# Gated products of a feed-forward on GpSimd in place of VectorE, with a copy by ScalarE

## Chip, cores and metric

One core of one Trainium2 chip. The metric is the device time of one execution in microseconds. The core has five queues that matter here: TensorE (PE in the profile; PEld are its weight loads), VectorE (DVE), ScalarE (ACT), GpSimd (POOL) and SyncE (SP), which issues the DMAs. Each runs its instructions strictly in order and waits for the others on semaphores.

## What is computed

`x` is 8 sequences of 512 tokens of width 128, float32. First comes a recurrent layer (`h = tanh(h A' + x B')`, output `h C'`, with layer norms and a residual), 512 steps one after the other. Then six layers, each of a local attention and a gated feed-forward:

```python
for i in range(DEPTH):                                   # DEPTH = 6
    x = attn_layer(shift_tokens(x), Wqkv[i], q_scale[i], k_scale[i], Wo[i]) + x
    x = ffn_layer(shift_tokens(x), ln_g[i], ln_b[i], W1[i], b1[i], W2[i], b2[i]) + x

def attn_layer(x, Wqkv, qs, ksc, Wo):                    # 16 heads of 64, windows of 32 tokens
    q, k, v = split(x @ Wqkv)
    q, k = rotate(l2norm(q) * qs), rotate(l2norm(k) * ksc)
    return local_attention(q, k, v) @ Wo                 # softmax over this window and the one before

def ffn_layer(x, g, bln, W1, b1, W2, b2):                # inner width 341
    xn = layernorm(x) * g + bln
    a, gate = jnp.split(xn @ W1 + b1, 2, -1)
    return a * jax.nn.gelu(gate, approximate=False) @ W2 + b2
```

## The kernel before

The order of the work is written out by hand for each engine; there is no planner. After the recurrence (about the first 400 us of the span) all six layers run as one software pipeline over 192 attention tiles (`NT`): 6 layers x 8 chunks of 64 tokens x 4 tiles; a tile is 4 sequences x 32 tokens = 128 rows. On each engine `step(s)` does one stage each of up to four tiles: A = s (projection of q and k, rotation, squares), B = s - 1 (normalised q and k transposed, scores, maximum), C = s - 2 (exponential, sum, weighting, product with the inputs), E = s - 3 (the output projection L597 and its addition to the residual). Four tiles are a turn T: 512 columns (8 sequences x 64 tokens, `CH`) that then go through the feed-forward. `turn_of(s, lag)` gives the turn whose feed-forward stage with that lag falls in step s:

- s mod 4 = 3, lag 7 and 11: rows transposed (L522), statistics on VectorE (`statistics`, L877, L881), small sums on GpSimd (L433, L435), and of the turn before, value product 0 (L544, then `glu`, L869).
- s mod 4 = 0, lag 8 and 12: GpSimd's shift (L408), ScalarE's normalised rows (L724); of the turn before, value products 1 and 2 (L544, `glu`).
- s mod 4 = 1, lag 9 and 13: transposed back and scaled (L529, L730); of the turn before, the output product (L551) and VectorE's update of the residual (`update`, L887).
- s mod 4 = 2, lag 6 and 10: the feed-forward's input is copied (L698); the gates (L537) and their Gelu on ScalarE (`gelu`, L741).

The inner width of 341 is held in three pieces of 128, 128 and 85 partitions (`FT`), so each turn has three gates `ge`, three values and three products `hh`, each 512 columns wide. Values come from TensorE in PSUM: `VALUES = ((11, 0, 2), (12, 1, 1), (12, 2, 2))` gives lag, piece and bank. PSUM has eight banks. Banks 4 to 7, named G(0) to G(3), are shared in each step by the transposed q and k (L509), the feed-forward's products, and the product with the inputs (L657). So L657 of tile C must wait until each bank has been read by its feed-forward user (`ffn_left`, called ahead of the first matmul into each bank, in the order 3, 0, 1, 2). `glu` on VectorE reads the value from PSUM, adds the bias, multiplies by the gate and writes `hh`; it counts `glu_done`, for which TensorE waits in `ffn_left` and ahead of L551.

VectorE's order in a step: rotation of q (L845, L848), sum of the exponentials (L906) and its reciprocal (L909), square sum of q (L854), residual (L914), rotation of k (L845, L848), transpose of the weights (L921), statistics, `glu` 0 or `glu` 1, `update`, square sum of k (L854), maximum of the scores (L938), `glu` 2, subtraction of the maximum (L944), inverse roots (L859 and L55 to L65, eleven small instructions one behind the other). ScalarE's: L749 (empties what L657 wrote), inputs L698, exponential L755, square of q (L709), L760, transposed q and k out of PSUM (L770, L775), `gelu` 0, square of k (L709), `ffn`. GpSimd's: shift L408, q and k times inverse roots (L414), weights (L419), q and k rotations added (L424), tables (L397), small sums (L433, L435). The inverse roots wait for L433 where there are statistics in the step (`variance_done`).

Of the kernel before, what the change touches and what calls it, by code (L numbers as in the profile page):

```python
# [104 lines left out]
def build(nc, a):  # L105
    with ExitStack() as ctx:
        def sb(name, shape, dt=F32):
            return ctx.enter_context(nc.sbuf_tensor(name, shape, dt))

        def sem(name):  # L110
            return ctx.enter_context(nc.semaphore(name))
# [45 lines left out]
        nmean = sb("nmean", [P, TB])  # L157
        ge = sb("ge", [P, 3, CH])
        hh = sb("hh", [P, 3, CH])

        mask_f = ex
        flat = cosp.rearrange("p a c n -> p (a c n)")
# [88 lines left out]
        gate_done = sem("gate_done")  # L251
        gelu_done = sem("gelu_done")
        a_done = sem("a_done")
        glu_done = sem("glu_done")
        fy_done = sem("fy_done")
        x_updated = sem("x_updated")
# [6 lines left out]
        def tile(n):  # L263
            return 0 <= n < NT

        def turn_of(s, lag):
            T = (s - lag) // ROUND
            return T if (s - lag) % ROUND == 0 and 0 <= T < TURNS else None

# [112 lines left out]
        @block.gpsimd  # L382
        def _(eng):
            eng.memset(xa[:, :, 0:1], 0.0).then_inc(zeroed, 1)
            eng.memset(xb[:, :, 0:1], 0.0).then_inc(zeroed, 1)
            eng.memset(hb[:, 1, FW - 1, :], 0.0).then_inc(zeroed, 1)
            eng.memset(kT[:, :, :, :, :], 0.0).then_inc(zeroed, 1)
            eng.memset(xtm[:, :, :, :], 0.0).then_inc(zeroed, 1)

            for c in range(NC):  # L390
                eng.wait_ge(h_done, FW * c + FW)
                after(eng, hs_turned, c)
                eng.tensor_copy(hs.rearrange("p (b t) -> p b t", b=BATCH), hb[:, c % 2, :, :].rearrange("p t b -> p b t")).then_inc(hs_done, 1)

            def scale_table(w, T):
                eng.wait_ge(tab_in[w], 32 * (T + 1))
                eng.tensor_tensor(tab[:, w, :, :], tab[:, w, :, :], qks[:, w, :, :], ALU.mult).then_inc(tab_ready[w], 1)  # L397

            scale_table(0, 0)

            def step(s):
                A, B, C = s, s - 1, s - 2
                T = turn_of(s, 8)
                if T is not None:
                    eng.wait_ge(norm_step, normed(s) if s <= NT else normed(s) + NSTEPS + 1)
                    after(eng, xn_ready, TB * T)
                    eng.wait_ge(variance_done, 2 * T + 2)
                    eng.tensor_tensor(shift[:, :], nmean[:, :], rr[:, 1, 2 * HEADS:], ALU.mult).then_inc(shift_done, 1)  # L408
                if tile(B):
                    eng.wait_ge(norm_step, normed(B + 1))  # L410
                    for i in range(2):
                        eng.wait_ge(rot_added, 2 * B + i + 1)
                        v = cosp[:, B % 2, i, :].rearrange("p (h d) -> p h d", d=DH)
                        eng.tensor_tensor(v, v, rr[:, B % 2, HEADS * i:HEADS * i + HEADS].unsqueeze(2).to_broadcast([P, HEADS, DH]),  # L414
                                          ALU.mult).then_inc(rot_ready, 1)
                if tile(C):
                    eng.wait_ge(recip_done, C + 1)
                    after(eng, p_turned, C)
                    eng.tensor_tensor(pn[:, :].rearrange("p (h k) -> p h k", k=DH), ex[:, :].rearrange("p (h k) -> p h k", k=DH),  # L419
                                      rsum[:, :].unsqueeze(2).to_broadcast([P, HEADS, DH]), ALU.mult).then_inc(weighed, 1)  # L420
                if tile(A):
                    for i, roped in enumerate((q_roped, k_roped)):
                        eng.wait_ge(roped, 2 * A + 2)
                        eng.tensor_tensor(cosp[:, A % 2, i, :], cosp[:, A % 2, i, :], sinp[:, i, :], ALU.add).then_inc(rot_added, 1)  # L424
                    if A % ROUND == 1:
                        scale_table(1, A // ROUND)
                    if A % ROUND == 3 and A + 1 < NT:
                        scale_table(0, A // ROUND + 1)
                T = turn_of(s, 7)
                if T is not None:  # L430
                    eng.wait_ge(stat_step, 2 * TB * T + 2 * TB)
                    after(eng, norm_step, normed(s))
                    eng.tensor_scalar(ss[:, 2 * HEADS:], aggr[:, :, 1], EPS, None, ALU.add).then_inc(variance_done, 1)  # L433
                    after(eng, shift_done, T)
                    eng.tensor_scalar(nmean[:, :], aggr[:, :, 0], -1.0, None, ALU.mult).then_inc(variance_done, 1)  # L435

            for s in range(LAST):
                step(s)

        @block.tensor  # L440
        def _(eng):
# [112 lines left out]
            def ffn_left(s, k):  # L554
# [9 lines left out]
                for lag, m, bank in VALUES:  # L564
                    T = turn_of(s, lag)
                    if T is not None and k == bank:
                        eng.wait_ge(glu_done, 3 * T + m + 1)
                T = turn_of(s, 13)
                if T is not None and k == 2:
                    eng.wait_ge(x_updated, NC + T + 1)  # L570
# [99 lines left out]
        def _(eng):  # L670
# [65 lines left out]
            def gelu(T, m):  # L736
# [3 lines left out]
                eng.wait_ge(gate_done, 3 * T + m + 1)  # L740
                eng.activation(ge[0:fn, m, :], G(GATE_BANKS[m])[0:fn], ACT.Gelu, bias=vec[0:fn, 6 + m:7 + m]).then_inc(gelu_done, 1)  # L741

            def step(s):
                A, B, C, E = s, s - 1, s - 2, s - 3
                if tile(E):
# [30 lines left out]
                T = turn_of(s, 10)  # L776
                if T is not None:
                    gelu(T, 0)
                if tile(A):
                    square(A, 1)  # L780
                ffn(s)
# [19 lines left out]
        def _(eng):  # L801
# [58 lines left out]
                eng.wait_ge(norm_step, base + 1)  # L860
                rsqrt(eng, ss[:, lo:hi], rbits[:, lo:hi], rhalf[:, lo:hi], rr[:, s % 2, lo:hi], norm_step, base + 1)

            def glu(T, m, k):
                fn = FT[m][1]
                eng.wait_ge(w1_in, 16 * DMA_W1 * (T // NC + 1))
                eng.wait_ge(a_done, 3 * T + m + 1)
                eng.wait_ge(gelu_done, 3 * T + m + 1)
                after(eng, fy_done, T)
                eng.scalar_tensor_tensor(out=hh[0:fn, m, :], in0=G(k)[0:fn], scalar=vec[0:fn, 3 + m:4 + m], in1=ge[0:fn, m, :],  # L869
                                         op0=ALU.add, op1=ALU.mult).then_inc(glu_done, 1)  # L870

            def statistics(T):
                base = 2 * TB * T
                eng.wait_ge(rows_done, T + 1)
# [22 lines left out]
            def step(s):  # L897
# [20 lines left out]
                if tile(C):  # L918
                    eng.wait_ge(weighed, C + 1)
                    after(eng, px_done, 4 * C)  # L920
                    eng.transpose(pT[:, :], pn[:, :]).then_inc(p_turned, 1)  # L921
                T7, T11, T12, T13 = turn_of(s, 7), turn_of(s, 11), turn_of(s, 12), turn_of(s, 13)
                if T7 is not None:
                    statistics(T7)
                if T11 is not None:
                    glu(T11, 0, 2)
                if T12 is not None:
                    glu(T12, 1, 1)
                if T13 is not None:
                    update(T13)  # L930
                c = leaving(s)
# [4 lines left out]
                if tile(B):  # L936
                    eng.wait_ge(sims_done, B + 1)
                    eng.tensor_reduce(mx[:, :], S, AX_X, ALU.max).then_inc(max_done, 1)  # L938
                if T12 is not None:
                    glu(T12, 2, 2)  # L940
                if tile(B):
                    eng.wait_ge(max_done, B + 1)
                    after(eng, exp_done, B)
# [76 lines left out]
```

## Time and profile before

| | us |
|---|---|
| timed runs, median of 3 (lowest, highest) | 3785.27 (3783.42, 3791.43) |
| the profiled execution | 3787.83 |
| its span, first to last instruction | 3786.0 |
| TensorE busy | 3558.4 |
| VectorE busy | 3058.2 |
| GpSimd busy | 2086.7 |
| ScalarE busy | 2037.8 |
| mean granted clock of TensorE | 0.969 of full speed |

Busy time is the sum of an engine's instructions; matmuls are pipelined, so a busy TensorE may still be a slow one. The profile puts an engine's idle time down to what released it: the instruction of another engine whose semaphore came last, or "issue" where nothing of the kind is seen. The timeline gives start and duration of merged instructions, the granted clock is a mean over the stretch asked for, 1.00 being full speed.

### The profile page before, as it was taken

Reading aid. Unit: us, or ns where it says so; the run is one execution under the profiler, and the core shown is the slowest. Engines: PE = TensorE matmul, PEld = TensorE weight load, DVE = VectorE, ACT = ScalarE, POOL = GpSimd, SP = SyncE. Lnnn points to the kernel's source line nnn. Section 1 sums busy time; section 2 is a strip of 40 time slices with the busy share of each in tenths; the row PEclk is TensorE's granted clock in tenths of the full one; section 3 lists DMA queues with packets and bytes.
Section 4 is the critical chain, followed back from the end, with each engine's and each line's share of the span. In section 5 each row is a group of like instructions: output and inputs, shape, how many; then the busy total and the mean of one; then the engine's idle time right before and its main releaser. Section 6 shows DMA issues by size and latency. Waiting matters only on the chain.

```text
span 3786.0 us, 101581 instructions
## 1 busy us (share of the span) xinstructions
PE 3558.4 (94%) x42643; PEld 2250.6 (59%) x42643; DVE 3058.2 (81%) x5670; ACT 2037.8 (54%) x3871; POOL 2086.7 (55%) x1217
## 2 busy tenths in 40 slices
PE   8999699999999999999999999999999999999997
PEld 4555366666665666666665666666656666566664
DVE  3443698888898888888888898888888888888884
ACT  2222356565565565565655655656556556556553
POOL 0000376666566666666665666666666666666662
PEclk9999899999999999999999999999999999999998
DMA  2000000000001000001000001000001000000000
GB/s 66 1 1 1 7 10 12 28 10 10 9 14 32 10 10 7 10 16 29 10 10 10 7 16 32 10 7 10 10 15 31 10 10 7 14 12 16 10 10 12
DMA packets 62283, 52.55 MB, mean 14 GB/s; under 512 B 11526, under 2 KB 59396, under 8 KB 61828
## 3 DMA queue, kind: packets, MB, share of 16 engines
q1 hardware_dynamic: 61828, 46.05, 4.6%
q8 instruction: 338, 5.54, 0.6%
q14 instruction: 117, 0.96, 0.1%
HBM read 43.93 MB, written 2.10 MB: 12 GB/s over the span
## 4 chain that ended last, share of the span: by engine, by line
PE 62%; DVE 19%; issue 11%; POOL 5%; ACT 2%; DVEq 0%; DMA 0%; SPq 0%; POOLq 0%; ACTq 0%
PE ps L502 16%; PE ps L597 12%; PE ps L657 7%; PE ps L469 6%; PE ps L509 6%; DVE sinp L848 4%; DVE mx L938 3%; PE ps L643 3%; PE ps L551 3%; DVE pT L921 3%; PE ps L485 3%; PE ps L537 3%; POOL cosp L424 2%; POOL cosp L414 2%; DVE ss L854 2%
## 5 line engine op out<-in xcount | busy, mean ns | idle before, releaser
L414 POOL TENSOR_TENSOR cosp<-cosp,rr 128x1024 f32<-128x1024 f32 x384 | 722.5, 1902 | 823.1 <-DVE rr L65 823.0
L424 POOL TENSOR_TENSOR cosp<-cosp,sinp 128x1024 f32<-128x1024 f32 x384 | 904.7, 2368 | 96.1 <-DVE sinp L848 95.5
L502 PE MATMUL ps<-w_qk,xs 128*128 128x512 f32 x1536 | 814.9, 656 | 19.8 <-ACT sq L709 14.2
L597 PEld LDWEIGHTS ps<-px,w_vo 128*128 128x128 f32 x6144 | 729.5, 197 | 155.2 <-issue 118.7
L597 PE MATMUL ps<-px,w_vo 128*128 128x128 f32 x6144 | 739.6, 280 | 22.9 <-issue 18.4
L709 ACT ACTIVATE sq<-ps 128x1024 f32<-128x1024 f32 x384 | 393.1, 1024 | 571.3 <-DVE sinp L848 571.3
L845 DVE TENSOR_TENSOR cosp<-ps,tab 128x1024 f32<-128x1024 f32 x384 | 469.6, 1223 | 267.6 <-PE ps L502 267.4
L749 ACT COPY px<-ps 128x512 f32<-128x512 f32 x768 | 398.8, 598 | 431.0 <-PE ps L657 428.2
L657 PE MATMUL ps<-pT,xtm 32*128 32x512 f32 x3072 | 539.6, 629 | 88.3 <-DVE hh L869 74.7
L502 PEld LDWEIGHTS ps<-w_qk,xs 128*128 128x128 f32 x1536 | 279.9, 203 | 403.5 <-issue 401.8
L854 DVE TENSOR_REDUCE ss<-sq 128x16 f32<-128x1024 f32 x384 | 455.6, 1187 | 60.9 <-ACT sq L709 60.5
L848 DVE TENSOR_TENSOR sinp<-ps,tab 128x1024 f32<-128x1024 f32 x384 | 466.3, 1214 | 0.0
L509 PEld LDWEIGHTS ps<-ident,cosp 128*128 128x128 f32 x3072 | 352.2, 142 | 159.4 <-issue 101.0
L509 PE MATMUL ps<-ident,cosp 128*128 128x128 f32 x3072 | 403.4, 275 | 43.5 <-POOL cosp L414 31.1
L419 POOL TENSOR_TENSOR pn<-ex,rsum 128x1024 f32<-128x1024 f32 x192 | 365.1, 1902 | 98.1 <-DVE rsum L909 98.1
L657 PEld LDWEIGHTS ps<-pT,xtm 32*128 32x128 f32 x3072 | 202.1, 184 | 274.4 <-DVE hh L869 113.2
L775 ACT COPY kT<-ps 128x512 f32<-128x512 f32 x384 | 206.1, 589 | 279.4 <-PE ps L509 279.4
L643 PEld LDWEIGHTS ps<-kT,qT 64*32 64x32 f32 x24576 | 254.6, 105 | 84.5 <-issue 78.0
L469 PE MATMUL ps<-ident_bf 128*128 128x512 bf16 x1024 | 303.8, 377 | 0.0
L643 PE MATMUL ps<-kT,qT 64*32 64x64 f32 x24576 | 286.0, 226 | 2.2 <-ACT kT L775 2.1
L485 PEld LDWEIGHTS ps<-cosp,qT 128*128 128x128 f32 x1024 | 154.0, 189 | 166.4 <-ACT cosp L688 156.1
L921 DVE STREAM_TRANSPOSE pT<-pn 128x1024 f32<-128x1024 f32 x192 | 237.0, 1234 | 3.5 <-POOL pn L419 3.5
(101 smaller groups left out, 4094.2 us busy)
## 6 DMA issues: line engine op xcount, KB each, us to landing
tab<-in_tab SPq DMA_DIRECT2D x96, 128.0 KB, 2.0
qks<-in_scales SPq DMA_DIRECT2D x96, 128.0 KB, 3.2
w_qk<-in_L_ffn_Wqkv SPq DMA_DIRECT2D x12, 512.0 KB, 6.9
w_v<-in_wv_t SPq DMA_DIRECT2D x6, 512.0 KB, 8.7
w_o<-in_L_ffn_Wo SPq DMA_DIRECT2D x6, 512.0 KB, 9.1
x<-in_L_attn_x SPq DMA_DIRECT2D x16, 128.0 KB, 3.4
out<-w_v SPq DMA_DIRECT2D x16, 128.0 KB, 2.4
w<-in_L_ffn_W SPq DMA_DIRECT2D x6, 341.0 KB
```

What stands on the lines that cost most here:

```text
L414: eng.tensor_tensor(v, v, rr[:, B % 2, HEADS * i:HEADS * i + HEADS].unsqueeze(2).to_broadcast([P, HEADS, DH]), ALU.mult).then_inc(rot_read ...
L424: eng.tensor_tensor(cosp[:, A % 2, i, :], cosp[:, A % 2, i, :], sinp[:, i, :], ALU.add).then_inc(rot_added, 1)
L469: eng.matmul(ps[:, 7, 0:KEEP].rearrange("p (a n) -> p a n", n=P), ident_bf[:, :], ident_bf[:, :].unsqueeze(1).to_broadcast([P, KEEP // P, ...
L502: t = eng.matmul(ps[:, u, :], xs[:, n % ROUND, :], w_qk[:, n // TILES % 2, i, 512 * u:512 * u + 512], start=True, stop=True)
L509: t = eng.transpose(G(k)[:, 128 * m:128 * m + 128], cosp[:, n % 2, i, at:at + 128], ident[:, :])
L597: t = eng.matmul(S0, w_vo[:, i // HP, i % HP, :], px[:, i, :], start=i == 0, stop=i == HEADS - 1)
L643: t = eng.matmul(ps[32 * b:32 * b + 32, 2 + h2, DH * hp:DH * hp + DH], qT[rows, hp, 32 * b:32 * b + 32], kT[rows, B % NG, hp, b, :], start ...
L657: t = eng.matmul(G(b), xtm[rows, C % NG, k, :], pT[rows, :].rearrange("p (h k q) -> p h k q", k=2, q=WIN)[:, :, k, :], start=k == 0, stop= ...
L749: eng.copy(px[:, :, 32 * b:32 * b + 32], G(b).rearrange("p (h q) -> p h q", q=WIN)).then_inc(px_evac, 1)
L845: eng.tensor_tensor(cosp[:, n % 2, i, :].rearrange("p (h d) -> p h d", d=DH), src, cos, ALU.mult).then_inc(roped, 1)
L848: eng.tensor_tensor(sinp[:, i, :].rearrange("p (h u f) -> p h u f", u=2, f=32), swapped, sin, ALU.mult).then_inc(roped, 1)
L854: eng.tensor_reduce(ss[:, HEADS * i:HEADS * i + HEADS], sq[:, i, :].rearrange("p (h d) -> p h d", d=DH), AX_X, ALU.add).then_inc(ssq_done, 1)
```

## The change

The buffer `aa` is added in SBUF. ScalarE copies each value with its bias from PSUM into `aa` (`value`, an Identity activation), behind its copies of q and k and ahead of the square of k, and counts `a_out`. GpSimd multiplies `aa` by the gate `ge` into `hh`, behind its additions for q and k and its table product, and counts `glu_done`. `glu` leaves VectorE. TensorE's `ffn_left` waits for `a_out` in place of `glu_done`; its wait ahead of L551 stays on `glu_done`. No DMA is added or moved; the load of W1 still waits for `glu_done`.

```diff
--- before.py
+++ after.py
@@ -157,6 +157,7 @@
         nmean = sb("nmean", [P, TB])
         ge = sb("ge", [P, 3, CH])
         hh = sb("hh", [P, 3, CH])
+        aa = sb("aa", [P, 3, CH])
 
         mask_f = ex
         flat = cosp.rearrange("p a c n -> p (a c n)")
@@ -251,6 +252,7 @@
         gate_done = sem("gate_done")
         gelu_done = sem("gelu_done")
         a_done = sem("a_done")
+        a_out = sem("a_out")
         glu_done = sem("glu_done")
         fy_done = sem("fy_done")
         x_updated = sem("x_updated")
@@ -426,6 +428,14 @@
                         scale_table(1, A // ROUND)
                     if A % ROUND == 3 and A + 1 < NT:
                         scale_table(0, A // ROUND + 1)
+                for lag, m, k in VALUES:
+                    T = turn_of(s, lag)
+                    if T is not None:
+                        fn = FT[m][1]
+                        eng.wait_ge(a_out, 3 * T + m + 1)
+                        eng.wait_ge(gelu_done, 3 * T + m + 1)
+                        after(eng, fy_done, T)
+                        eng.tensor_tensor(hh[0:fn, m, :], aa[0:fn, m, :], ge[0:fn, m, :], ALU.mult).then_inc(glu_done, 1)
                 T = turn_of(s, 7)
                 if T is not None:
                     eng.wait_ge(stat_step, 2 * TB * T + 2 * TB)
@@ -564,7 +574,7 @@
                 for lag, m, bank in VALUES:
                     T = turn_of(s, lag)
                     if T is not None and k == bank:
-                        eng.wait_ge(glu_done, 3 * T + m + 1)
+                        eng.wait_ge(a_out, 3 * T + m + 1)
                 T = turn_of(s, 13)
                 if T is not None and k == 2:
                     eng.wait_ge(x_updated, NC + T + 1)
@@ -740,6 +750,13 @@
                 eng.wait_ge(gate_done, 3 * T + m + 1)
                 eng.activation(ge[0:fn, m, :], G(GATE_BANKS[m])[0:fn], ACT.Gelu, bias=vec[0:fn, 6 + m:7 + m]).then_inc(gelu_done, 1)
 
+            def value(T, m, k):
+                f0, fn = FT[m]
+                eng.wait_ge(w1_in, 16 * DMA_W1 * (T // NC + 1))
+                eng.wait_ge(a_done, 3 * T + m + 1)
+                after(eng, glu_done, 3 * T)
+                eng.activation(aa[0:fn, m, :], G(k)[0:fn], ACT.Identity, bias=vec[0:fn, 3 + m:4 + m]).then_inc(a_out, 1)
+
             def step(s):
                 A, B, C, E = s, s - 1, s - 2, s - 3
                 if tile(E):
@@ -776,6 +793,10 @@
                 T = turn_of(s, 10)
                 if T is not None:
                     gelu(T, 0)
+                for lag, m, k in VALUES:
+                    T = turn_of(s, lag)
+                    if T is not None:
+                        value(T, m, k)
                 if tile(A):
                     square(A, 1)
                 ffn(s)
@@ -859,15 +880,6 @@
                 eng.tensor_scalar(ss[:, lo:hi], ss[:, lo:hi], 1e-24, None, ALU.max).then_inc(norm_step, 1)
                 eng.wait_ge(norm_step, base + 1)
                 rsqrt(eng, ss[:, lo:hi], rbits[:, lo:hi], rhalf[:, lo:hi], rr[:, s % 2, lo:hi], norm_step, base + 1)
-
-            def glu(T, m, k):
-                fn = FT[m][1]
-                eng.wait_ge(w1_in, 16 * DMA_W1 * (T // NC + 1))
-                eng.wait_ge(a_done, 3 * T + m + 1)
-                eng.wait_ge(gelu_done, 3 * T + m + 1)
-                after(eng, fy_done, T)
-                eng.scalar_tensor_tensor(out=hh[0:fn, m, :], in0=G(k)[0:fn], scalar=vec[0:fn, 3 + m:4 + m], in1=ge[0:fn, m, :],
-                                         op0=ALU.add, op1=ALU.mult).then_inc(glu_done, 1)
 
             def statistics(T):
                 base = 2 * TB * T
@@ -919,13 +931,9 @@
                     eng.wait_ge(weighed, C + 1)
                     after(eng, px_done, 4 * C)
                     eng.transpose(pT[:, :], pn[:, :]).then_inc(p_turned, 1)
-                T7, T11, T12, T13 = turn_of(s, 7), turn_of(s, 11), turn_of(s, 12), turn_of(s, 13)
+                T7, T13 = turn_of(s, 7), turn_of(s, 13)
                 if T7 is not None:
                     statistics(T7)
-                if T11 is not None:
-                    glu(T11, 0, 2)
-                if T12 is not None:
-                    glu(T12, 1, 1)
                 if T13 is not None:
                     update(T13)
                 c = leaving(s)
@@ -936,8 +944,6 @@
                 if tile(B):
                     eng.wait_ge(sims_done, B + 1)
                     eng.tensor_reduce(mx[:, :], S, AX_X, ALU.max).then_inc(max_done, 1)
-                if T12 is not None:
-                    glu(T12, 2, 2)
                 if tile(B):
                     eng.wait_ge(max_done, B + 1)
                     after(eng, exp_done, B)
```

## Rows read from the trace of the kernel before

**Rows 1.** The page, part 1: busy time, share of the span and instructions of each engine.

```profile
PE 3558.4 (94%) x42643; PEld 2250.6 (59%) x42643; DVE 3058.2 (81%) x5670; ACT 2037.8 (54%) x3871; POOL 2086.7 (55%) x1217
```

**Rows 2.** Timeline (start us, us, engine line op out<-in xcount), the output update, three successive turns.

```profile
2149.95 0.75 DVE L887 SCALAR_TENSOR_TENSOR xa<-ps,vec,xb 128x512 f32<-128x512 f32 x1 [0.46 <-PE ps L551]
...
2216.85 0.75 DVE L887 SCALAR_TENSOR_TENSOR xa<-ps,vec,xb 128x512 f32<-128x512 f32 x1 [0.47 <-PE ps L551]
...
2287.08 0.75 DVE L887 SCALAR_TENSOR_TENSOR xa<-ps,vec,xb 128x512 f32<-128x512 f32 x1 [0.46 <-PE ps L551]
...
2355.67 0.75 DVE L887 SCALAR_TENSOR_TENSOR xa<-ps,vec,xb 128x512 f32<-128x512 f32 x1 [0.46 <-PE ps L551]
```

**Rows 3.** Timeline of TensorE: an update step's L657, then a value step; [idle before <-releaser].

```profile
2009.41 2.00 PE L657 MATMUL ps<-pT,xtm 32*128 32x512 f32 x16
...
2054.00 1.88 PE L544 MATMUL ps<-xf,w 128*128 128x512 f32 x4
...
2057.65 1.13 PE L657 MATMUL ps<-pT,xtm 32*128 32x512 f32 x6
...
2060.43 2.27 PE L657 MATMUL ps<-pT,xtm 32*128 32x512 f32 x10 [1.64 <-DVE hh L869]
...
2062.63 3.35 PE L502 MATMUL ps<-w_qk,xs 128*128 128x512 f32 x4
```

**Rows 4.** Waits: who waited for whom, us in total, times, longest us.

```profile
PE ps L657 <- DVE hh L869: 74.7, 46, 1.6
```

**Rows 5.** Windows: start:end, length, busy time of each engine, granted clock (PEclk), DMA share, GB/s.

```profile
2062.60:2066.00 3.40, 3.40 (x7) 1.58 (x7) 1.26 (x7) 2.63 (x6) 1.85 (x1) 0.59 0.03 5
```

**Rows 6.** Timeline of ScalarE, VectorE and GpSimd, a statistics step.

```profile
2038.93 1.02 ACT L709 ACTIVATE sq<-ps 128x1024 f32<-128x1024 f32 x1 [0.88 <-DVE sinp L848]
...
2041.05 0.75 DVE L869 SCALAR_TENSOR_TENSOR hh<-ps,vec,ge 128x512 f32<-128x512 f32 x1
...
2041.71 1.21 DVE L854 TENSOR_REDUCE ss<-sq 128x16 f32<-128x1024 f32 x1
...
2042.20 0.23 POOL L433 TENSOR_SCALAR ss<-aggr 128x4 f32<-128x4 f32 x1
```

**Rows 7.** Timeline of VectorE, the value step that follows.

```profile
2056.76 0.71 DVE L869 SCALAR_TENSOR_TENSOR hh<-ps,vec,ge 128x512 f32<-128x512 f32 x1
...
2057.39 1.21 DVE L854 TENSOR_REDUCE ss<-sq 128x16 f32<-128x1024 f32 x1
...
2059.64 0.74 DVE L869 SCALAR_TENSOR_TENSOR hh<-ps,vec,ge 85x512 f32<-85x512 f32 x1
...
2060.30 1.21 DVE L944 TENSOR_TENSOR sh<-ps,mx 128x1024 f32<-128x1024 f32 x1
```

**Rows 8.** Groups by line: xcount | busy us, mean ns | idle before us <-releasers.

```profile
L424 POOL TENSOR_TENSOR cosp<-cosp,sinp 128x1024 f32<-128x1024 f32 x384 | 904.7, 2368 | 96.1 <-DVE sinp L848 95.5
...
L741 ACT ACTIVATE ge<-ps,vec 128x512 f32<-128x512 f32 x144 | 93.1, 687 | 1.6 <-PE ps L537 1.0
...
L397 POOL TENSOR_TENSOR tab<-tab,qks 128x256 f32<-128x256 f32 x96 | 70.0, 729 | 0.0
...
L730 ACT ACTIVATE xf<-ps,vec 128x512 f32<-128x512 f32 x48 | 37.1, 772 | 1.7 <-PE ps L529 1.7
```

**Rows 9.** Timeline of ScalarE and GpSimd, the same value step.

```profile
2053.73 4.70 POOL L424 TENSOR_TENSOR cosp<-cosp,sinp 128x1024 f32<-128x1024 f32 x2
...
2055.72 1.02 ACT L709 ACTIVATE sq<-ps 128x1024 f32<-128x1024 f32 x1 [0.88 <-DVE sinp L848]
...
2064.14 3.76 POOL L414 TENSOR_TENSOR cosp<-cosp,rr 128x1024 f32<-128x1024 f32 x2 [5.72 <-DVE rr L65]
```

**Rows 10.** Timeline of VectorE, L845 in a value step at full clock.

```profile
2195.57 1.22 DVE L845 TENSOR_TENSOR cosp<-ps,tab 128x1024 f32<-128x1024 f32 x1 [0.52 <-PE ps L502]
...
2206.61 1.23 DVE L845 TENSOR_TENSOR cosp<-ps,tab 128x1024 f32<-128x1024 f32 x1 [0.31 <-PE ps L502]
...
2212.88 1.23 DVE L845 TENSOR_TENSOR cosp<-ps,tab 128x1024 f32<-128x1024 f32 x1 [1.23 <-PE ps L502]
```

## Prediction, written before the changed kernel was run

> **What bounds the kernel now.** I read the page first, then the groups by line, then the waits, then the instructions in order of time for one turn, and last the granted clock of short stretches. On the page [rows 1] TensorE is busy for 94% of the span; but a busy TensorE is not one at full speed, and the same row has VectorE at 81%. So I looked at whole turns (four steps of the pipeline, one feed-forward turn in them). The output update at L887 runs once a turn, and its starts [rows 2] give the length of three successive turns: 2216.85 - 2149.95 = 66.90 us, then 70.23, then 68.59. Leaving aside turns that load a new layer and the last ones, whose steps also turn results out, all come in these three lengths: one fixed schedule with something of 0, about 1.67 or about 3.32 us on top.
>
> I name the steps by the feed-forward work in them: gate step (L537, L741), statistics step (L877, value product 0), value step (value products 1 and 2), update step (L551, L887). The extra time is all in the value step. There TensorE's last product of attention, L657, is cut in two [rows 3]: six matmuls start at 2057.65, ten at 2060.43, after 1.64 us of idling "<-DVE hh L869". In the waits this pair is 74.7 us in 46 waits [rows 4]: it happens in every turn. What comes behind it differs: in that turn the next projection L502 takes 3.35 us, and the stretch 2062.6 to 2066 has a granted clock of 0.59 of full speed [rows 3, 5], that is a mixture of the 2.4 GHz level and the 1.2 GHz level. The engine had been idle for 1.64 us just before the fall. So the feed-forward products on VectorE cost twice: TensorE waits for them, and in most turns it then runs slow for some us, in which VectorE waits for TensorE.
>
> **What the change removes from the statistics step.** The one L869 there starts at 2041.05 and the next square sum L854 at 2041.71 [rows 6]: 0.66 us of VectorE's queue. From there to the next step VectorE doesn't idle, so all of it should come off the step if nothing else becomes late. ScalarE gets the value copy in front of the square of k. That square runs from 2038.93 to 2039.95 [rows 6]; behind a copy of 0.7 us it ends near 2040.6, and L854 can start at 2041.05 at the earliest, so nearly 0.5 us remain. 45 such steps: 45 x 0.66 = 29.7 us.
>
> **What it removes from the value step.** Here VectorE has two L869: 2056.76 to 2057.39 = 0.63, and 2059.64 to 2060.30 = 0.66 us of its queue [rows 7]. The second stands behind the maximum in VectorE's queue, and TensorE's L657 needs bank 2 empty: that is the stall. After the change L657 waits for ScalarE's copy. TensorE's four L544 matmuls for both values run from 2054.00 to 2055.88 [rows 3]; the first copy can start near 2055.0, the second near 2056.0. A copy is an ACTIVATE with a bias from PSUM: L741 with a Gelu takes 687 ns, L730 with bias and scale 772 [rows 8]. I take 0.69 and keep 0.77 as the long end; the second, ending near 2056.7, is done 0.95 us before L657 starts at 2057.65. So L657 runs in one piece, 2.00 us as in the update step [rows 3], and there is no stall.
>
> The price is that the square of k, which starts at 2055.72 and takes 1.02 us [rows 9], now starts behind both copies, near 2056.65, and ends near 2057.7. VectorE's L854 needs it. It started at 2057.39; without the first product it would be ready at 2056.76, but now waits until 2057.7, that is 0.31 us later than today. The second product's 0.66 us then come off: 0.35 us earlier at L944, of which I keep 0.3, since the maximum is then read by the very next instruction. So of 1.29 us taken from VectorE in this step only 0.3 are won there, and 0.94 turn into a wait for ScalarE. (With a copy of 0.77 us the win is 0.2; if the copies delay nothing, 1.29.)
>
> Now the TensorE side, first in a turn at full clock. From L845 for k at 2195.57 to the same in the next step at 2212.88 are 17.31 us [rows 10]. In it VectorE waits for TensorE 0.31 us at 2206.61 and 1.23 at 2212.88, where 0.52 is the ordinary wait at this place (the first of these rows); both waits come from the late L657. Without the stall 17.31 - 0.31 - (1.23 - 0.52) = 16.29, less 0.3 = 15.99 us. So 1.32 us a turn, 45 turns: 59.4 us. Next limits: after L657, ScalarE's normalising activations L724 end about 1 us later than now (the copies before them), and L749, which empties what L657 writes, can begin when L657 ends; by my estimate TensorE is then ready for the next step about 0.5 us before VectorE needs it. Little, but enough.
>
> Then the clock. I counted the value steps by length, from L845 to L845: of 45, 10 have 17.3 us, 19 have 19.0 and 16 have 20.6 (the differences are those of the turns in rows 2). If the clock doesn't fall any more, 19 x 1.67 + 16 x 3.32 = 84.8 us are won. TensorE's other, shorter waits are there now in the turns that keep their clock as well, so I expect no fall from them.
>
> **What it adds to GpSimd.** Three tensor-tensor products of 512 columns a turn. L424 (both inputs full tensors, 1024 columns) takes 2368 ns, L397 (256 columns) 729 [rows 8]. A line through both is 0.18 us + 2.13 ns a column, 1.27 us for 512; half of L424 is 1.18, twice L397 1.46, the two ends. They stand behind both L424. In the value step these end at 2053.73 + 4.70 = 2058.43, the two products at 2061.0; the next need of GpSimd is L414 at 2064.14, 0.35 earlier after the change [rows 9]. Nearly 3 us are to spare. In the statistics step the product stands behind L424 and L397 and ahead of L433, whose result VectorE's inverse root waits for: L433 started at 2042.20 [rows 6] and starts near 2043.5 now. VectorE needs it after L854, L938 and L944; in the value step these take 2060.30 - 2057.39 - 0.66 = 2.25 us up to L944 and 1.21 for that one [rows 7], so near 2041.05 + 3.46 = 2044.5. Some 0.8 us are to spare when L433 itself is added. The products' reader, L551, comes a step later. I cost all three at nothing. The cover in the statistics step is the thinner one: a product of over 2.1 us would show there.
>
> The Trainium skill ("SBUF — State Buffer", "Who interferes with whom") speaks against moving work there: a VectorE instruction with two SBUF inputs and a GpSimd instruction that reads SBUF exclude one another for the whole instruction. No row of before has the two at once. In VectorE's order only the small instructions of the inverse roots (L61 to L65) have two such inputs, and they start 0.8 us after the products' end. By the rule nothing changes unless the products are later than worked out; that is the second rival.
>
> **Ends of the run.** In the last two turns nothing hides the products: copy and product in a row (0.69 + 1.27) for 0.73, the second product behind the first. I add 2.5 us.
>
> **Sum.** 29.7 + 59.4 + 84.8 - 2.5 = 171.4 us. The profiled execution took 3787.83 us around a span of 3786.0; the three timed runs have a median of 3785.27, 2.6 us lower; I take the sum off the median: 3785.3 - 171.4 = 3614 us, 4.5% faster.
>
> **Rivals.** (1) The clock still falls, though the stall is gone. For it: the stall alone doesn't decide it, since 10 of the 45 value steps have the same stall and keep the clock. Against: all slow L502 that I found stand behind the cut L657. Of the 84.8 us some 0.5 us a fall are then hidden by the slack found above, 35 x 0.5 = 17; so 68 us are not won: 3682 us. Chance 0.14.
> (2) GpSimd's products fall on VectorE's inverse roots, or the two hold each other up, up to one product a turn: 48 x 1.27 = 61 us less won, 3675 us. For it: GpSimd's queue is in order and a product could start late. Against: the margins of 0.8 us. Chance 0.06.
> (3) Slower than before: GpSimd becomes the bound. A product of X us delays the statistics step by X - 2.1 and the value step, with two, by 2X - 5.4. The gain of 171.4 / 48 = 3.6 us a turn is used up at 3X - 7.5 = 3.6, X = 3.7 us; at X = 4 the kernel takes 48 x 0.9 = 43 us more, 3828. Against it stand L424 and L397: X is three times what they give. Chance 0.03.
> (4) The change doesn't do what it says: L657 goes on waiting at the same place, for ScalarE's copies, since they are later than I make them by more than 2.5 us, and the time stays within 0.2%. For it nothing but the longer queue of ScalarE, which is 54% busy [rows 1]. Chance 0.02.
>
> **How the numbers follow.** The forecast holds with 0.75. Its own spread: copies at 0.77 us cost 5 us, the square not being late would win 45 x 1.0 = 45, but needs TensorE to be early as well (at most the 0.5 us, 22 us): 3592 to 3625. The range reaches to both middling rivals: 3592 to 3690. Differences under 0.2% (about 8 us) can't be told from none. Faster 0.95, same 0.02, slower 0.03.
>
> **What would show it.** L657 in one piece of 16 matmuls in the value step, and no wait of it for VectorE; granted clock near 1.00 through the value step; L869 gone from VectorE, a new wait of L854 for the square of nearly 1 us once a turn; GpSimd products near 1.27 us with no wait of L414 or of the inverse roots behind them; turns of one length near 66.9 - 1.3 - 0.66 = 64.9 us. It would be wrong if slow projections remained, if L657 waited for a copy, or if the inverse roots waited for L433.

## The result

The changed kernel takes 3610.27 us (median of 4 runs, 3609.73 to 3610.63) against 3785.3 before: a ratio of 0.9535, 95% interval 0.9518 to 0.9551. The forecast was 3614 us. Span 3608.3 us, mean granted clock 0.992 in place of 0.969. The page, part 1 (busy us, share, instructions), against rows 1 of before:

```profile
PE 3439.6 (95%) x42643; PEld 2181.2 (60%) x42643; DVE 2965.6 (82%) x5526; ACT 2116.0 (59%) x4015; POOL 2260.2 (63%) x1361
```

VectorE lost 93 us of work, ScalarE and GpSimd got 78 and 174. TensorE's busy time fell by 119 us though it does the same 42643 matmuls; by lines, L657 went from 539.6 to 459.0 us and the projection from 814.9 to 761.1. Only a part of that is the clock: in `e4_filled` below, at full clock but with L657 still waiting, the two have 515.0 and 757.8 us. The rest of L657's fall is that its matmuls no longer wait in between. The output update L887 is now L899; three of its starts (start us, us), answering to rows 2:

```profile
1862.18 0.75 DVE L899 SCALAR_TENSOR_TENSOR xa<-ps,vec,xb 128x512 f32<-128x512 f32 x1 [0.46 <-PE ps L561]
...
1926.95 0.75 DVE L899 SCALAR_TENSOR_TENSOR xa<-ps,vec,xb 128x512 f32<-128x512 f32 x1 [0.46 <-PE ps L561]
...
1991.68 0.75 DVE L899 SCALAR_TENSOR_TENSOR xa<-ps,vec,xb 128x512 f32<-128x512 f32 x1 [0.46 <-PE ps L561]
```

64.77 and 64.73 us: the turns have one length now (those that load a new layer and the last ones apart), where before they had 66.9, 68.6 or 70.2. From the first update to the 45th the run of before took 3045.8 us, this one 2870.3: 175.5 us for 44 turns, 3.99 a turn.

A value step of the changed kernel, from its timeline (start us, us, engine, line), answering to rows 3, 7 and 9. L554 are the value matmuls, L758 the copies, L438 the products, L719 the square, L875 the square sum, L667 what was L657, L512 the projection, L880 the first instruction of the inverse roots, L866 the next rotation:

```profile
1972.48 1.88 PE L554 MATMUL ps<-xf,w 128*128 128x512 f32 x4
...
1973.60 0.69 ACT L758 ACTIVATE aa<-ps,vec 128x512 f32<-128x512 f32 x1 [0.27 <-issue]
...
1974.45 0.68 ACT L758 ACTIVATE aa<-ps,vec 85x512 f32<-85x512 f32 x1 [0.17 <-PE ps L554]
...
1975.04 1.01 ACT L719 ACTIVATE sq<-ps 128x1024 f32<-128x1024 f32 x1
...
1976.08 1.22 DVE L875 TENSOR_REDUCE ss<-sq 128x16 f32<-128x1024 f32 x1 [0.76 <-ACT sq L719]
...
1976.14 2.00 PE L667 MATMUL ps<-pT,xtm 32*128 32x512 f32 x16
...
1976.85 2.51 POOL L438 TENSOR_TENSOR hh<-aa,ge 128x512 f32<-128x512 f32 x2
...
1978.07 1.98 PE L512 MATMUL ps<-w_qk,xs 128*128 128x512 f32 x4
...
1978.47 1.22 DVE L950 TENSOR_TENSOR sh<-ps,mx 128x1024 f32<-128x1024 f32 x1
...
1979.61 0.17 DVE L880 TENSOR_SCALAR ss<-ss 128x32 f32<-128x32 f32 x1
...
1982.16 1.22 DVE L866 TENSOR_TENSOR cosp<-ps,tab 128x1024 f32<-128x1024 f32 x1
```

The reader is to see three things. L667 runs in one piece of 16 matmuls and the projection behind it takes 1.98 us, not 3.35: no stall, full clock. L875 has a new wait of 0.76 us for the square that now stands behind the copies. And GpSimd's two products end at 1979.36, only 0.25 us before VectorE's L880 starts. The statistics step, answering to rows 6:

```profile
1957.96 0.69 ACT L758 ACTIVATE aa<-ps,vec 128x512 f32<-128x512 f32 x1 [0.71 <-issue]
...
1960.22 1.18 DVE L875 TENSOR_REDUCE ss<-sq 128x16 f32<-128x1024 f32 x1
1961.33 1.21 DVE L946 TENSOR_REDUCE mx<-ps 128x16 f32<-128x1024 f32 x1
...
1961.28 1.27 POOL L438 TENSOR_TENSOR hh<-aa,ge 128x512 f32<-128x512 f32 x1
...
1962.63 0.23 POOL L443 TENSOR_SCALAR ss<-aggr 128x4 f32<-128x4 f32 x1
...
1963.71 0.17 DVE L880 TENSOR_SCALAR ss<-ss 128x36 f32<-128x36 f32 x1
```

L875 follows the statistics without a wait, and L443 ends 0.85 us before L880 needs it. The granted clock over 1000 us in the middle (the column behind POOL's) is full:

```profile
1500.00:2500.00 1000.00, 976.27 (x12978) 630.22 (x12977) 897.79 (x1616) 642.62 (x1114) 723.59 (x436) 1.00 0.06 15
```

### The profile page after: what moved, and what is told of

It reads as the page before. It is cut to its first block and busy times, and to the rows that moved or that the text cites. A ratio compares the mean times of both kernels' runs of the same rounds, so it can differ in the third digit from the quotient of the medians.

```text
span 3608.3 us, 101728 instructions
## 1 busy us (share of the span) xinstructions
PE 3439.6 (95%) x42643; PEld 2181.2 (60%) x42643; DVE 2965.6 (82%) x5526; ACT 2116.0 (59%) x4015; POOL 2260.2 (63%) x1361
## 5 line engine op out<-in xcount | busy, mean ns | idle before, releaser
L426 POOL TENSOR_TENSOR cosp<-cosp,sinp 128x1024 f32<-128x1024 f32 x384 | 903.2, 2369 | 56.7 <-DVE sinp L869 56.0
L607 PEld LDWEIGHTS ps<-px,w_vo 128*128 128x128 f32 x6144 | 705.5, 192 | 167.6 <-issue 88.8
L512 PE MATMUL ps<-w_qk,xs 128*128 128x512 f32 x1536 | 761.1, 618 | 35.9 <-ACT sq L719 30.3
L607 PE MATMUL ps<-px,w_vo 128*128 128x128 f32 x6144 | 727.7, 277 | 37.4 <-issue 32.9
L719 ACT ACTIVATE sq<-ps 128x1024 f32<-128x1024 f32 x384 | 392.0, 1021 | 462.7 <-DVE sinp L869 462.7
L866 DVE TENSOR_TENSOR cosp<-ps,tab 128x1024 f32<-128x1024 f32 x384 | 469.3, 1222 | 139.1 <-PE ps L512 138.3
L875 DVE TENSOR_REDUCE ss<-sq 128x16 f32<-128x1024 f32 x384 | 455.1, 1185 | 94.8 <-ACT sq L719 94.8
L512 PEld LDWEIGHTS ps<-w_qk,xs 128*128 128x128 f32 x1536 | 262.7, 191 | 398.9 <-issue 397.2
L667 PE MATMUL ps<-pT,xtm 32*128 32x512 f32 x3072 | 459.0, 616 | 8.8 <-DVE pT L933 4.7
L519 PE MATMUL ps<-ident,cosp 128*128 128x128 f32 x3072 | 404.9, 275 | 28.2 <-POOL cosp L416 15.9
L667 PEld LDWEIGHTS ps<-pT,xtm 32*128 32x128 f32 x3072 | 171.9, 184 | 156.2 <-issue 86.8
L698 ACT ACTIVATE cosp<-ps 128x8 f32<-128x8 f32 x512 | 90.7, 177 | 259.4 <-PE ps L495 259.4
```

Of the source, the lines that this page charges most:

```text
L512: t = eng.matmul(ps[:, u, :], xs[:, n % ROUND, :], w_qk[:, n // TILES % 2, i, 512 * u:512 * u + 512], start=True, stop=True)
L519: t = eng.transpose(G(k)[:, 128 * m:128 * m + 128], cosp[:, n % 2, i, at:at + 128], ident[:, :])
L607: t = eng.matmul(S0, w_vo[:, i // HP, i % HP, :], px[:, i, :], start=i == 0, stop=i == HEADS - 1)
L667: t = eng.matmul(G(b), xtm[rows, C % NG, k, :], pT[rows, :].rearrange("p (h k q) -> p h k q", k=2, q=WIN)[:, :, k, :], start=k == 0, stop= ...
L719: eng.activation(sq[:, i, :], R.rearrange("p a n -> p (a n)"), ACT.Square).then_inc(sq_done, 1)
L866: eng.tensor_tensor(cosp[:, n % 2, i, :].rearrange("p (h d) -> p h d", d=DH), src, cos, ALU.mult).then_inc(roped, 1)
```

## Experiments

**Is it the place of the wait, or the work on VectorE?** `e1_order` is the kernel before with one move in VectorE's order:

```diff
                 if T12 is not None:
                     glu(T12, 1, 1)
+                    glu(T12, 2, 2)
...
                 if tile(B):
                     eng.wait_ge(sims_done, B + 1)
                     eng.tensor_reduce(mx[:, :], S, AX_X, ALU.max).then_inc(max_done, 1)
-                if T12 is not None:
-                    glu(T12, 2, 2)
```

> The kernel before, with one move on VectorE: product 2 stands directly behind product 1, ahead of the square sum of k, not behind the maximum. All products stay on VectorE. Theory (the gain came mostly from L657 no longer waiting for the late product, and the clock with it): product 2 is ready near 2058.1 in the time of the value step shown, L657 is all but whole, no slow L502; value step 16.3 us, turn 65.9 us, about 3655 us in all. Rival (the gain came from VectorE having less to do): VectorE does as much as before, so near 3785 us, or 3700 at best if only the clock comes back.

Measured: 3657.87 us (3655.42 to 3658.82), ratio 0.9653 (0.9637 to 0.9669); its turns are 65.9 us. The theory holds, the rival falls: with all three products still on VectorE, 128.8 us of the 176 are won by the order alone. In its value step TensorE's L657 is in one piece again, 2.50 us in place of 1.13, a wait of 1.64 and 2.27, and the projection behind it runs at full clock (timeline of `e1_order`):

```profile
2001.32 2.50 PE L657 MATMUL ps<-pT,xtm 32*128 32x512 f32 x16
2003.74 1.98 PE L502 MATMUL ps<-w_qk,xs 128*128 128x512 f32 x4
```

The value step has 16.3 us, as expected.

**What does the clock cost, and what brings it down?** `e4_filled` leaves the kernel before as it is and gives TensorE something to do while it waits:

```diff
+                    if turn_of(s, 12) is not None and tile(B):
+                        for _ in range(FILL):                      # FILL = 8
+                            eng.matmul(G(3).rearrange("p (a n) -> p a n", n=P), ident_bf[:, :],
+                                       ident_bf[:, :].unsqueeze(1).to_broadcast([P, CH // P, P]), start=True, stop=True)
                     for k in range(2):
                         for b in (3, 0, 1, 2):
```

> The kernel before with 8 small bf16 matmuls (some 1.7 us, results overwritten) ahead of L657 in each value step: the same wait for VectorE's product 2, but TensorE works while it waits. Theory (the fall of the clock follows the idle 1.64 us): no slow L502, every value step 17.3 us, 85 us less than before: 3700 us. Rival (the fall has another cause, or the stretch is too busy already): 3785 us.

Measured: 3702.74 us (3702.61 to 3703.68), ratio 0.9773 (0.9757 to 0.9789); turns of 66.9 us all through, the shortest of the three lengths of before. The timeline of its value step:

```profile
2021.83 1.90 PE L655 MATMUL ps<-ident_bf 128*128 128x512 bf16 x8
2023.66 2.92 PE L662 MATMUL ps<-pT,xtm 32*128 32x512 f32 x16
2026.51 1.98 PE L503 MATMUL ps<-w_qk,xs 128*128 128x512 f32 x4
```

Work that is thrown away makes the kernel 84 us faster. L662 (the former L657) still waits for product 2, as its 2.92 us show, but the projection L503 takes 1.98 us and over 2900 us the clock stays at 1.00. So the fall followed TensorE's idling, and it cost what the turn lengths said: 84 against 84.8 us. Why the same wait left the clock alone in 10 of 45 value steps before, no run here shows.

**The wait put back.** `e3_late_bank` is the changed kernel with TensorE again waiting for the product, now GpSimd's:

```diff
                     if T is not None and k == bank:
-                        eng.wait_ge(a_out, 3 * T + m + 1)
+                        eng.wait_ge(glu_done, 3 * T + m + 1)
```

> The changed kernel with one wait put back: L657 takes a bank only when GpSimd's product is done (as before it waited for VectorE's), not when ScalarE's copy is. Theory: L657 is cut in the value step until 3.3 us after its start and in the statistics step too, 2 us; the clock falls behind them; turn 70 to 72 us, 3835 to 3925 us, slower than the kernel before. Rival (less work on VectorE is what counts): 3610 to 3660 us.

Measured: 3895.72 us (3890.88 to 3903.95), ratio 1.0289 (1.0263 to 1.0314), slower than before. Its TensorE in a statistics step (first two lines) and in the value step behind it:

```profile
2025.34 3.70 PE L667 MATMUL ps<-pT,xtm 32*128 32x512 f32 x10 [0.78 <-POOL hh L438]
2028.97 3.61 PE L512 MATMUL ps<-w_qk,xs 128*128 128x512 f32 x4
...
2044.98 4.99 PE L667 MATMUL ps<-pT,xtm 32*128 32x512 f32 x12 [0.61 <-POOL hh L438]
2049.90 3.39 PE L512 MATMUL ps<-w_qk,xs 128*128 128x512 f32 x4
```

Both projections run at low clock, and turns have 67.3 to 74.3 us. The shortest are only 0.4 us longer than the shortest of before, so most of the loss is the clock. Without the early release by ScalarE's copy, moving the products to GpSimd would have lost 109 us.

**The copy without the move.** `e2_copy_only` keeps the copies and the early release, but multiplies on VectorE:

```diff
-                        eng.tensor_tensor(hh[0:fn, m, :], aa[0:fn, m, :], ge[0:fn, m, :], ALU.mult).then_inc(glu_done, 1)   # GpSimd
+            def glu(T, m):                                        # VectorE, at the places of before
...
+                eng.tensor_tensor(hh[0:fn, m, :], aa[0:fn, m, :], ge[0:fn, m, :], ALU.mult).then_inc(glu_done, 1)
```

> The changed kernel with its copies by ScalarE and its early release of the banks, but the product (copy times gate) on VectorE, at the places it had before. Theory: no stall of L657, full clock; VectorE has its 0.66 us in the statistics step and 0.66 in the value step back: turn 66.0 us, about 3665 us. Port rule as a rival (a VectorE instruction with two SBUF inputs and a GpSimd instruction that reads SBUF exclude one another): products 0 and 1 fall into L424 and wait for its end, 1.0 and 1.4 us more a turn, about 3770 us, or L424 grows longer by as much.

Measured: 3727.22 us (3726.64 to 3728.69), ratio 0.9838 (0.9822 to 0.9854), turns of 67.4 us, between the two. The timeline shows why. Product 1 (value step) beside GpSimd's two L426, then product 2 with GpSimd idle, all in the first fence; the second has product 0 beside L399 (statistics step):

```profile
2027.82 4.70 POOL L426 TENSOR_TENSOR cosp<-cosp,sinp 128x1024 f32<-128x1024 f32 x2
...
2030.85 2.21 DVE L881 TENSOR_TENSOR hh<-aa,ge 128x512 f32<-128x512 f32 x1
...
2035.25 0.67 DVE L881 TENSOR_TENSOR hh<-aa,ge 85x512 f32<-85x512 f32 x1
```

```profile
2014.92 0.96 DVE L881 TENSOR_TENSOR hh<-aa,ge 128x512 f32<-128x512 f32 x1
...
2015.29 1.19 POOL L399 TENSOR_TENSOR tab<-tab,qks 128x256 f32<-128x256 f32 x1
```

Product 1 takes 2.21 us and ends at 2033.06, half a microsecond behind L426's end at 2032.52; product 2, the same width, takes 0.67. In the statistics step product 0 waits for the end of the second L426 too (2010.64 + 4.70 = 2015.34), and then L399 takes 1.19 us instead of 0.73, its end 0.6 us behind product 0's. Each engine waits for the other's whole instruction. By the Trainium skill ("SBUF — State Buffer", "Who interferes with whom") that is an exclusive lock between a VectorE instruction with two SBUF inputs and a GpSimd instruction reading SBUF; the trace agrees. The two products last 1.5 and 0.3 us longer for it, and a turn 1.4 us longer than the theory's 66.0. The fused form of before reads the value from PSUM and has none of this: its 0.71 us at 2056.76 lie beside L424 [rows 7, 9]. So the copy without the move is still 59 us faster than before, by the early release, but 69 us slower than `e1_order`, which needs no copy.

**Where does GpSimd become the bound?** `e5_double` and `e6_triple` do each product two and three times, the extra ones into a spare buffer:

```diff
+                        for i in range(EXTRA):                     # 1 in e5_double, 2 in e6_triple
+                            after(eng, spare_done, EXTRA * (3 * T + m) + i)
+                            eng.tensor_tensor(spare[0:fn, :], aa[0:fn, m, :], ge[0:fn, m, :], ALU.mult).then_inc(spare_done, 1)
                         eng.tensor_tensor(hh[0:fn, m, :], aa[0:fn, m, :], ge[0:fn, m, :], ALU.mult).then_inc(glu_done, 1)
```

> The changed kernel, each product on GpSimd done twice (the first into a spare buffer): 2.55 us in place of 1.27. Theory by the margins of the prediction (2.1 us in the statistics step, 5.4 us for two in the value step): only the statistics step grows, since L433 and with it the inverse roots come 0.45 us late; 45 x 0.45 = 20 us, 3630 us. Rival (VectorE and GpSimd exclude one another where both read SBUF for a second operand): in the value step the products now lie beside the inverse roots too, and VectorE's small instructions wait for up to a product, 1.0 to 1.3 us more a turn: 3675 to 3690 us.

Measured: 3765.42 us (3762.18 to 3770.2), ratio 0.9948 (0.9931 to 0.9965). Both expectations are far too low. The timeline of its value step (L443, L444 the products, L886 and L55 the first two instructions of the inverse roots, L525 the transposes of the next step):

```profile
2049.89 1.26 POOL L443 TENSOR_TENSOR spare<-aa,ge 85x512 f32<-85x512 f32 x1
2051.12 1.27 POOL L444 TENSOR_TENSOR hh<-aa,ge 85x512 f32<-85x512 f32 x1
...
2050.17 1.02 DVE L886 TENSOR_SCALAR ss<-ss 128x32 f32<-128x32 f32 x1
2051.23 1.20 DVE L55 TENSOR_SCALAR rbits<-ss 128x32 int32<-128x32 int32 x1
2052.46 0.18 DVE L57 TENSOR_SCALAR rr<-rbits 128x32 int32<-128x32 int32 x1
...
2056.71 1.09 PE L525 MATMUL ps<-ident,cosp 128*128 128x128 f32 x8 [1.86 <-POOL cosp L419]
```

L886, 0.17 us in the changed kernel, lasts until the third of the four products ends; L55 until the fourth ends: they grow by 0.85 + 1.02 = 1.87 us, and the value step by 1.82. These instructions have one input each, in SBUF. So the exclusion is not confined to two inputs, as the prediction took it; the Trainium skill (the same section) names tensor_scalar among the operations that can take the shared ports, and the trace agrees. The statistics step grows by 0.55 us, where 0.45 was worked out. TensorE now idles 1.86 us at L525, and the two turn lengths, 67.1 and 68.8 us, differ by the 1.67 us of a clock fall. From the first update to the 45th the turns are 140 us longer in all: 104 by 2.37 us each, and 36 by the falls, which neither expectation had.

> The changed kernel, each product done three times: 3.85 us. The prediction put the point at which the whole gain is used up at 3.7 us. Theory (GpSimd is then the bound, statistics step 1.75 and value step 2.1 us longer): 3610 + 45 x 3.85 = 3783 us. Rival (exclusion of VectorE by GpSimd's reads on top): the inverse roots of the value step wait for a product in each gap, over 3830 us.

Measured: 3934.51 us (3933.29 to 3934.99), ratio 1.0389 (1.0369 to 1.0408): the rival's side. Turns of 71.7 us, 6.9 more than in the changed kernel and not 3.85. In the value step shown, the third of its six products (L443, L444) ends at 2057.29; its last three, then the inverse roots:

```profile
2057.25 2.65 POOL L443 TENSOR_TENSOR spare<-aa,ge 85x512 f32<-85x512 f32 x2
2059.86 1.26 POOL L444 TENSOR_TENSOR hh<-aa,ge 85x512 f32<-85x512 f32 x1
...
2056.23 1.10 DVE L886 TENSOR_SCALAR ss<-ss 128x32 f32<-128x32 f32 x1
2057.36 1.20 DVE L55 TENSOR_SCALAR rbits<-ss 128x32 int32<-128x32 int32 x1
2058.59 0.18 DVE L57 TENSOR_SCALAR rr<-rbits 128x32 int32<-128x32 int32 x1
2058.81 1.13 DVE L61 TENSOR_TENSOR rhalf<-rr 128x32 f32<-128x32 f32 x1
2059.98 1.19 DVE L63 SCALAR_TENSOR_TENSOR rhalf<-rhalf,ss 128x32 f32<-128x32 f32 x1
```

Four instructions, two with one tensor input and two with two, each last until a product ends: 3.9 us longer than alone, taken together. L57 slips in between two products here; in one value step it is L57 that waits, 1.20 us at 2562.95. TensorE then idles 3.87 us, and VectorE waits 1.1 us longer than usual for the slow projection behind that. Together that is the 5.0 us by which the value step grows; the statistics step grows by 1.9, since L886 waits 1.79 us there for the small sums. So the prediction's break-even of 3.7 us for a product lies too high; at 2.55 us the gain is down to 23 us (3788.9 in this comparison before), so it is little above that.

**A better place for the square.** `e7_square_first` is the changed kernel with two blocks exchanged on ScalarE:

```diff
+                if tile(A):
+                    square(A, 1)
                 for lag, m, k in VALUES:
                     T = turn_of(s, lag)
                     if T is not None:
                         value(T, m, k)
-                if tile(A):
-                    square(A, 1)
```

> The changed kernel with the square of k ahead of the value copies on ScalarE. Theory: the wait of L854 for the square in the value step (0.76 us in the changed kernel) is gone, the second copy is still done when L657 comes to its bank; TensorE and the emptying of its banks then limit, so some 0.7 us a turn: 3578 us. Rival (L657 waits for the copies instead and the stall and low clock come back): 3620 to 3700 us.

Measured: 3590.25 us (3589.95 to 3592.8), ratio 0.9481 (0.9463 to 0.9499), 20 us better than the changed kernel, where 32 were expected; its value step has 15.5 us in place of 15.9. Its timeline, products and inverse roots:

```profile
1965.96 2.50 POOL L438 TENSOR_TENSOR hh<-aa,ge 128x512 f32<-128x512 f32 x2
...
1967.87 0.63 DVE L880 TENSOR_SCALAR ss<-ss 128x32 f32<-128x32 f32 x1
1968.54 0.18 DVE L55 TENSOR_SCALAR rbits<-ss 128x32 int32<-128x32 int32 x1
```

VectorE is earlier by 0.8 us, comes into GpSimd's products, and gives 0.46 us back. `e9_half` tests that reading; it is `e7_square_first` with product 2 computed over half its columns only (the other half is left out, so it serves for timing alone):

```diff
+                        cols = CH if m < 2 else CH // 2
-                        eng.tensor_tensor(hh[0:fn, m, :], aa[0:fn, m, :], ge[0:fn, m, :], ALU.mult).then_inc(glu_done, 1)
+                        eng.tensor_tensor(hh[0:fn, m, 0:cols], aa[0:fn, m, 0:cols], ge[0:fn, m, 0:cols], ALU.mult).then_inc(glu_done, 1)
```

> As e7_square_first, with product 2 on GpSimd only over half its columns (the other half of its output is left out, zeros), 0.72 us in place of 1.27. It tells whether the 0.46 us that the first instruction of the inverse roots takes too long in e7_square_first is a wait for GpSimd's products. Theory (exclusion): that instruction takes 0.17 us again and a turn is 0.46 us shorter, 3590 - 21 = 3569 us. Rival (TensorE limits the value step anyway): 3585 to 3590 us.

Measured: 3573.26 us (3572.76 to 3574.43), 17 us less, where the reading gave 21: of the 0.46 us a turn 0.37 come off. L882 (the former L880) is short again, starting when the products are all but over:

```profile
1958.85 1.97 POOL L440 TENSOR_TENSOR hh<-aa,ge 128x512 f32<-128x512 f32 x2
...
1960.77 0.17 DVE L882 TENSOR_SCALAR ss<-ss 128x32 f32<-128x32 f32 x1
```

**Faster versions.** `e8_tail` is `e7_square_first` with the products of the last two turns given back to VectorE:

```diff
+TAIL = TURNS - 2
-                    if T is not None:
+                    if T is not None and T < TAIL:                 # ScalarE's value and GpSimd's product
...
-                        eng.wait_ge(a_out, 3 * T + m + 1)
+                        eng.wait_ge(a_out if T < TAIL else glu_done, 3 * T + m + 1)
```

> As e7_square_first, and the products of the last two turns back on VectorE, since nothing hides copy and product there. Theory: the 6 us that the end of the run grew by come back: 3572 us. Rival (the end is bound by TensorE at low clock either way): as e7_square_first.

Measured: 3585.58 us (3584.68 to 3589.57), ratio 0.947 (0.9451 to 0.9488): 4.7 us below e7_square_first, near the 6 expected. From its 46th update to the 48th are 41.0 us, as before, against 47.0 in the changed kernel. `e10_merged` is `e8_tail` with one instruction for products 1 and 2:

```diff
-                        eng.tensor_tensor(hh[0:fn, m, :], aa[0:fn, m, :], ge[0:fn, m, :], ALU.mult).then_inc(glu_done, 1)
+                    eng.tensor_tensor(hh[:, 1:3, :], aa[:, 1:3, :], ge[:, 1:3, :], ALU.mult).then_inc(glu_done, 2)
```

> As e8_tail, with products 1 and 2 as one GpSimd instruction over 1024 columns: 2.37 us by the row of L424 in place of 2.50 for two. Theory (the inverse roots wait for the end of the products): 0.13 us a turn, 3586 - 6 = 3580 us. Against it: one instruction can't be split, so whatever on VectorE comes into it waits for its whole rest; that would be the same end here.

Measured: 3578.76 us (3576.97 to 3580.7), ratio 0.9446 (0.9432 to 0.946), the fastest version that computes everything: 32 us below the changed kernel. Its turns have 64.2 us against 64.3.

## Why the prediction was right, and where it was off

- *The stall goes and the clock stays up (59.4 and 84.8 us).* Right in mechanism and size. The filled kernel measures the clock alone at 84 us; the reordered one measures clock, stall and what product 2's place cost together at 129 us. What is left to the changed kernel, 3657.9 - 3610.3 = 47.6 us, is VectorE's shorter queue: turns of 65.9 against 64.8 us, 51 us from the first update to the 45th, less what the longer end takes back.
- *The statistics step, 0.66 us.* 16.83 us before and 16.11 now, so 0.72; the margin for L433, 0.8 us, measured 0.85.
- *The value step, 15.99 us.* It has 15.89. The copies take 687 and 684 ns (0.69 was taken), and the wait of L854 for the square is 0.76 us where 0.94 was worked out. These two lines together are worth 0.16 us, about the difference of 3.99 and 3.86 us a turn, since 171.4 + 2.5 = 173.9 us over 45 turns are 3.86.
- *The product, 1.27 us.* Right to the digit; groups by line with the shapes apart, us busy, mean ns:

```profile
L438 POOL TENSOR_TENSOR hh<-aa,ge 128x512 f32<-128x512 f32 x96 | 122.3, 1274 | 35.3 <-ACT aa L758 35.1 <-issue 0.2
...
L758 ACT ACTIVATE aa<-ps,vec 128x512 f32<-128x512 f32 x96 | 66.0, 687 | 52.8 <-issue 48.8 <-PE ps L554 4.0
```

- *"I cost all three at nothing ... nearly 3 us are to spare" in the value step.* The time is right, the step behind it was incomplete, and only luck of 0.25 us hides it. It measured the margin to L414, and for the exclusion to L61, the first instruction with two SBUF inputs. VectorE's L859 and L55 exclude GpSimd as well and come first. The margin was 0.25 us, not 0.8. The kernels with longer products and the one with the earlier square show what lies behind it: 0.46 us where an inverse root comes in late in a product, 0.85 to 1.02 where it waits for nearly a whole one.
- *Rival 3, break-even at 3.7 us a product.* Wrong for the same cause, with the clock falls on top: at 2.55 us the kernel is only 0.5% faster than before, at 3.85 us 3.9% slower, where 4 us were to give 3828 us.
- *The ends, 2.5 us.* Mis-sized. From the last gates to the end of the run are 33.6 us before (3748.68 to 3782.26) and 39.5 now (3565.02 to 3604.49), 5.9 us more. The last turn of the changed kernel, products 1 and 2, then the output product, then the update:

```profile
3594.27 2.48 POOL L438 TENSOR_TENSOR hh<-aa,ge 128x512 f32<-128x512 f32 x2 [1.10 <-ACT aa L758]
...
3597.00 3.47 PE L561 MATMUL ps<-hh,w 128*128 128x512 f32 x4 [2.72 <-POOL hh L438]
...
3601.63 0.75 DVE L899 SCALAR_TENSOR_TENSOR xa<-ps,vec,xb 128x512 f32<-128x512 f32 x1 [9.41 <-PE ps L561]
```

TensorE idles 2.72 us for the products and then runs L561 slowly, 3.47 us for its first four matmuls where before all six took 2.82; the working had left that out.

Against the sum of the prediction: 175.5 us from the 1st update to the 45th, 3.0 before them, 5.2 from the 45th to the 46th, less 5.9 at the end, is to the rounding the 177.7 us by which the spans differ. Outside these 44 turns that is a gain of 2.3 us, where the sum had one more turn of 3.9 less 2.5: that the end, mis-sized by 3.4 us, hardly shows in the total is luck.

## What to carry to other kernels

When an engine waits for a shared bank, ask first who must read it last, and where that instruction stands in its queue: moving one product up in VectorE's order brought 129 of 176 us, and moving the work to another engine without an early release would have lost 109. A short idle time of TensorE is to be priced with the clock that follows it, from the different lengths of the same step in one trace. And before work goes to GpSimd, look at what VectorE does at that moment with operands in SBUF, one-input tensor_scalar instructions included, not only at the queue of GpSimd.

## What the runs showed of the hardware

- TensorE's clock fell behind idle times of 1.64 us and, in `e3_late_bank`, behind several shorter ones (0.78 and 0.61 us beside the cut L667), to projections of 3.4 to 3.8 us in place of 1.98; the same 1.64 us left it alone in 10 of 45 steps. Eight overwritten bf16 matmuls (1.90 us) in the idle time kept it up everywhere.
- VectorE's tensor-tensor with both inputs in SBUF waited out GpSimd's instruction (2.21 in place of 0.67 us), and GpSimd's waited out VectorE's (1.19 in place of 0.73 us).
- VectorE's tensor_scalar on 32 columns, one input, float32 (L880) and int32 (L55), did the same: 1.02 and 1.20 us in place of 0.17 and 0.18. In `e6_triple` up to four small instructions behind one another each waited so, 3.9 us in all.
